# Two attentions: query tiles of stride four, four wide turning products, and value products moved ahead of a score

## The reference

```python
# L2: 8 heads of 16, softmax attention; the heads of a channel are added, then a raw reshape
p = softmax(einsum('bhsd,bhtd->bhst', q, k) / sqrt(dk))
att = einsum('bhst,bhtd->bhsd', p, v)
out = att.reshape(S, B, D, H).sum(axis=-1).reshape(B, S, D)
# L3: 16 heads of 8, scanned over blocks of 64 keys with a running maximum m;
#     l_new = chunk_sum * corr + chunk_sum, so the last block's correction enters the denominator
out = flash(Q, K, V).transpose(0, 2, 1, 3).reshape(B, S, E) @ out_w.T + out_b
```

## Time and profile before

| | us |
|---|---|
| median of 3 runs | 3012.55 (3006.28 to 3018.29) |
| profiled execution, its own time | 3009.39 |
| its span on the core | 3007.6 |
| `sa` head loop, about | 1266 to 1742 |
| `ba` head loop, about | 1934 to 2812 |

### The profile page before, as it was taken

One profiled execution on the slowest core, in us unless ns is written; L12 is line 12 of the kernel. 1 busy time (PEld: TensorE's weight loads), 2 busy tenths in 40 slices (PEclk: granted clock), 3 DMA queues, 4 the chain that ended last, 5 costly groups with the idle time before them and its releaser, 6 DMA issues.

```text
span 3007.6 us, 61281 instructions
## 1 busy us (share of the span) xinstructions
PE 2345.3 (78%) x19700; PEld 1301.3 (43%) x19752; DVE 1890.4 (63%) x3795; ACT 1308.9 (44%) x2628; POOL 507.1 (17%) x941
## 2 busy tenths in 40 slices
PE   4369958788887785499999955489999999999855
PEld 3246634666665432234444433133333333333434
DVE  5857565655554476376666645477777777777281
ACT  4211144333332202156666633166666666666322
POOL 4402320333332002011111101000000000000013
PEclk9655567889998697599999977599999999999676
DMA  2232200000000001411111001411111111111000
GB/s 64 75 100 64 66 22 0 7 0 0 0 0 1 7 0 45 143 31 28 27 27 27 22 3 49 137 28 32 28 30 32 27 32 32 27 32 27 2 16 28
DMA packets 146722, 98.97 MB, mean 33 GB/s; under 512 B 61150, under 2 KB 126055, under 8 KB 146602
## 3 DMA queue, kind: packets, MB, share of 16 engines
q1 hardware_dynamic: 146602, 97.35, 12.1%
HBM read 56.85 MB, written 39.85 MB: 32 GB/s over the span
## 4 chain that ended last, share of the span: by engine, by line
PE 57%; DVE 19%; issue 9%; ACT 6%; SPq 5%; POOL 2%; DMA 2%; DVEq 1%; ACTq 0%; POOLq 0%; PEldq 0%
PE psum L2056 10%; PE psum L2044 9%; PE psum L2033 9%; PE psum L2068 6%; SPq L1970 4%; DVE X L1281 2%; PE psum L645 1%; DVE tt_sp L1687 1%; PE psum L405 1%; DVE dn_arena L925 1%; ACT ba_pt L2132 1%; PE psum L634 1%; PE psum L668 1%; PE psum L1604 1%; DVE tt_tsp L1685 1%
## 5 line engine op out<-in xcount | busy, mean ns | idle before, releaser
L2262 DVE TENSOR_REDUCE ba_blockmax<-psum 128x16 f32<-128x1024 f32 x512 | 608.9, 1221 | 183.1 <-PE psum L2033 182.6
L2132 ACT ACTIVATE ba_pt<-psum 128x512 f32<-128x512 f32 x1024 | 541.5, 603 | 272.7 <-PE psum L2044 272.6
L2264 DVE TENSOR_REDUCE sa_negmax<-psum 128x1 f32<-128x1024 f32 x256 | 304.4, 1221 | 151.3 <-PE psum L2033 150.9
L2044 PE MATMUL psum<-ba_qs,ba_ks 64*128 64x512 bf16 x1024 | 339.5, 383 | 72.0 <-DVEq L59 50.9
L2033 PE MATMUL psum<-ba_ks,ba_qs 64*128 64x512 bf16 x1024 | 347.1, 423 | 38.4 <-DMA ba_ks<-ba_kstk 30.6
L2132 ACT ACTIVATE sa_pt<-psum 128x512 f32<-128x512 f32 x512 | 268.2, 602 | 194.1 <-PE psum L2044 120.4
L2056 PE MATMUL psum<-ba_pt,ba_vh 128*32 128x512 f32 x2048 | 278.4, 616 | 0.2 <-ACT ba_pt L2132 0.2
L2033 PEld LDWEIGHTS psum<-ba_ks,ba_qs 64*128 64x128 bf16 x1024 | 123.6, 146 | 306.5 <-issue 301.5
L2033 PE MATMUL psum<-sa_ks,sa_qs 96*128 96x512 bf16 x512 | 207.7, 411 | 41.1 <-DMA sa_ks<-sa_kstk 30.4
L2044 PE MATMUL psum<-sa_qs,sa_ks 128*128 128x512 bf16 x460 | 174.4, 383 | 10.2 <-DVEq L59 8.2
L2044 PEld LDWEIGHTS psum<-ba_qs,ba_ks 64*128 64x128 bf16 x1024 | 77.1, 93 | 174.4 <-issue 150.2
(11 more groups left out here) (477 smaller groups left out, 4165.3 us busy)
## 6 DMA issues: line engine op xcount, KB each, us to landing
ba_qs<-ba_qstk SPq DMA_DIRECT2D x128, 96.0 KB, 2.1
ba_ks<-ba_kstk SPq DMA_DIRECT2D x128, 96.0 KB, 2.2
sa_qstk<-sa_pq SPq DMA_DIRECT2D x48, 128.0 KB
sa_kstk<-sa_pk SPq DMA_DIRECT2D x48, 128.0 KB
sa_qs<-sa_qstk SPq DMA_DIRECT2D x32, 192.0 KB, 2.6
sa_ks<-sa_kstk SPq DMA_DIRECT2D x32, 192.0 KB, 2.7
ba_qstk<-ba_pq SPq DMA_DIRECT2D x48, 128.0 KB, 2.3
ba_kstk<-ba_pk SPq DMA_DIRECT2D x48, 128.0 KB, 2.3
```

The source lines that it names most:

```text
L2044: nc.tensor.matmul(bank(4 + slot), ks[b][K0:P, x_ * P:(x_ + 1) * P], qs[b][K0:P, h * HALF:(h + 1) * HALF], start=True, stop=True).then_inc ...
L2132: nc.scalar.activation(pt[2 * x_ + h][:, :], bank(4 + slot), ACT.Exp, scale=SCALE).then_inc(pt_in, 1)
L2262: ins = nc.vector.tensor_reduce(blockmax[g][:, r, :], src.rearrange("p (n s) -> p n s", s=BLOCK), AXX, ALU.max, negate=True)
L2264: ins = nc.vector.tensor_reduce(negmax[g][:, r:r + 1], src, AXX, ALU.max, negate=True)
```

## The change

Query tile r no longer holds the queries `a * 8 + r` but `(r // 4) * 512 + a * 4 + r % 4`. What follows from that: the row scores' weights have a column step of 4, the maxima go to `qs` by two DMAs of half a row for each part (four values, 8 bytes, from each partition), and four products with 128 weight columns (step 4) and both halves of `sel` as moving data take the place of the 16 of `turn_out`. In `sa` the result is no longer in the token order of `X`; SyncE moves it there by two DMAs into a new buffer `moved`, after the `maxima` of its body, and POOL's `add` waits for these. In `project_out` the copy's output order changes. Besides, in odd key tiles the value products are issued between the second row score and the second key-major score.

```diff
+    moved = [k.sb(f"{tag}_moved{g}", [P, D], ctx=ctx) for g in range(3)] if not blocked else None
...
             for z in range(3):
-                s.dma_start(qs[b][MR + z:MR + z + 1, :], mparts[b][:, z, :]).then_inc(m_in[b], 16)
+                for h in range(2):
+                    s.dma_start(qs[b][MR + z:MR + z + 1, h * HALF:(h + 1) * HALF],
+                                mparts[b][:, z, h * GROUP:(h + 1) * GROUP]).then_inc(m_in[b], 16)
...
                 maxima(n.at(1))
+            if not blocked and c != 0:
+                move(n.at(-1))
+
+        def move(n):
+            b = n.c % 3
+            s.wait_ge(normed, n.of(1, 1))
+            k.plain(s)
+            for h in range(2):
+                s.dma_start(moved[b][h * (P // 2):(h + 1) * (P // 2), :], onorm[b][:, h * GROUP:(h + 1) * GROUP, :]).then_inc(moved_in[b], 16)
...
         heads(s, body)
+        if not blocked:
+            move(Head(0, N - 1))
...
-            last = nc.tensor.matmul(bank(2 * slot + h), qs[b][0:KP, :].rearrange("p (a r) -> p r a", r=NTB)[:, r, :],
+            mine = qs[b][0:KP, r // GROUP * HALF:(r // GROUP + 1) * HALF].rearrange("p (a m) -> p m a", m=GROUP)[:, r % GROUP, :]
+            last = nc.tensor.matmul(bank(2 * slot + h), mine,
...
-            for r in range(NTB):
-                for h in range(2):
-                    lhsT = oT[n.c % 3][:, :].rearrange("p (a r) -> p r a", r=NTB)[:, r, :]
-                    last = nc.tensor.matmul(k.psum[h * 64:(h + 1) * 64, 4 + slot, r * V1:(r + 1) * V1], lhsT, sel[:, h, :],
-                                            start=True, stop=True, skip_group_check=True)
+            out = bank(4 + slot)[:, 0:NTB * V1].rearrange("p (h m e) -> p m h e", h=2, m=GROUP)
+            for m in range(GROUP):
+                last = nc.tensor.matmul(out[:, m, :, :], oT[n.c % 3][:, :].rearrange("p (a m) -> p m a", m=GROUP)[:, m, :], sel[:, :, :],
+                                        start=True, stop=True, skip_group_check=True)
...
-                    t.wait_ge(m_in[n.c % 3], n.third(48, 49))
+                    t.wait_ge(m_in[n.c % 3], n.third(96, 97))
...
                 for h in range(2):
                     if ahead:
                         rows_scores(lead, r, h)
+                    if h == 1 and x_ == 1 and c != 0:
+                        values(n.at(-1), 3)
+                    if h == 1 and x_ in (3, 5, 7):
+                        values(n, (x_ - 3) // 2)
                     key_scores(n, x_, h)
-                if x_ == 1 and c != 0:
-                    values(n.at(-1), 3)
-                if x_ in (3, 5, 7):
-                    values(n, (x_ - 3) // 2)
...
-            p.wait_ge(normed, n.of(1, 1))
+            p.wait_ge(moved_in[n.c % 3], n.third(32, 32))
...
-            nc.gpsimd.tensor_tensor(xs, xs, onorm[n.c % 3][:, :, :].rearrange("p r e -> p (r e)"), ALU.add).then_inc(added, 1)
+            nc.gpsimd.tensor_tensor(xs, xs, moved[n.c % 3][:, :], ALU.add).then_inc(added, 1)
...
-                dst = oT[b % 2][:, :].rearrange("d (p r) -> d r p", r=NTB)[:, g * GROUP:(g + 1) * GROUP, :]
+                dst = oT[b % 2][:, g * GT:(g + 1) * GT].rearrange("d (p m) -> d m p", m=GROUP)
```

More of the change, by code:

```diff
@@ L1912, in attention @@
     normed, all_done = mk("normed"), mk("all_done")
+    moved_in = many("moved_in", 3)
     layer = k.layers
@@ L2172, in split_max @@
             if n.c >= 3:
-                p.wait_ge(m_in[g], n.third(48, 1))
+                p.wait_ge(m_in[g], n.third(96, 1))
             k.plain(p)
```

## The result

The changed kernel takes **3076.2 us** (median of 4 runs, 3064.8 to 3081.3), against 3015.1 for the kernel before on the same chip: ratio **1.020** (95% interval 1.017 to 1.024). It is slower by 2%, some 61 us. The prediction was 3001, with a range of 2950 to 3032.

A forecast was written before the change was run, and what follows sets the result against it. `sa` was taken as bound by TensorE, `ba` by TensorE and its waits, with the maxima's chain becoming binding. The terms -34.2 + 2.7 + 3.6 + 18.6 - 2.0 = -11.3 took the median from 3012.5 to 3001 us, range 2980 to 3022 (outer 2950 to 3032).

The forecast's parts named there:

- I take T + 5.5: In `ba`, the row maximum of key tile 4 starts 5.5 us after T, the start of key tile 0.
- 0.1 to TensorE: In `ba`, TensorE starts 0.1 us after the last DMA of the maxima lands.
- 18.6: In `ba`, the longer maxima chain makes the period 13.7 against 13.39: +0.3 for each of 62 periods, +18.6 us.
- rival 2: In `ba`, dearer issues (0.7) or landings 0.5 later make the period 14.2, total 3033 us; chance 0.17.
- I take 0.97 ... 1.07 us saved a head: The turning products, 2.04 us before, take 0.97 us as 8 passes, saving 1.07 us a head.
- -34.2 us in `sa`: In `sa`, bound by TensorE, cheaper turning products save 1.07 us in each of 32 heads: -34.2 us.
- rival 3: The turning products do not get cheaper, `sa` stays at 14.36 a head, total 3037 us; chance 0.06.
- 0 (a column of step 4 costs what keeps the total): Lower bound on the turning products' saving a head: 0, if step-4 columns keep their total time unchanged.
- the order at 0: Issuing value products earlier in odd key tiles changes nothing: 0 in `sa`, hidden by the maxima wait in `ba`.
- The clock, named as a danger without a price: In `ba`, a granted clock under 1.00 because TensorE rests 2 us at a time would prove the forecast wrong.
- I take no change: Row scores' weight loads at step 4, bounded by 140 and 93 ns, were taken as unchanged.
- rival 4: Row weights at step 4 load in 93 ns, making `ba`'s period 13.5 and the total 2990 us; chance 0.12.

The follow-up runs named there:

- experiment 2: The changed kernel with the maxima written by three DMAs of a whole row, as before, instead of six: 3017.8 us, ratio 1.0036.
- experiment 4: The changed kernel with VectorE's `negative` issued after the row maximum of key tile 3 instead of key tile 4: 3021.7 us, ratio 1.0063.
- experiment 1: The changed kernel with each turning product reading 128 adjacent columns of `oT` as weights: 3070.4 us, ratio 1.021.
- experiment 9: The changed kernel with `negative` at key tile 3 and ScalarE's copy laying out adjacent columns for the turning products: 2948.2 us, ratio 0.978.
- experiment 3: The changed kernel with the value products put back behind the second key-major score: 3125.8 us, ratio 1.040.
- experiment 6: The kernel before with only the new order, value products of odd key tiles ahead of the second key-major score: 3022.6 us, ratio 1.0029.
- experiment 7: The kernel before with only the turning products in their new wide form, 128 queries each with stride four: 3014.7 us, ratio 1.0011.
- experiment 8: The kernel before with ScalarE's copy laying each query tile's 64 columns side by side, turning products still in halves: 2984.4 us, ratio 0.991.

## Why the prediction was wrong

**Right: the mechanism in `ba`.** The chain from row maximum through POOL and six DMAs binds, TensorE waits for it, and each DMA costs 0.60 whatever its bytes. 3.14 and the landing came out as written, five issues at 3.08 for 2.98. Taking the chain's length away, in two ways (experiments 2 and 4), takes most of the loss away. Here the rule cited from the Trainium skill (DMA: Bandwidth & Descriptors, Rules for kernel authors) held: splitting doubled SP's time for the issues of a head, 1.77 to 3.70 us, on the path.

**Wrong by its size: the chain.** "I take T + 5.5" measured 5.94; five issues took 0.10 more and "0.1 to TensorE" measured 0.26, so the period is 14.42 and not 13.72. The start's 0.44 is 27 us over 62 heads and the rest 16, and `ba`'s periods as a whole, 67 us against 18.6, are the largest part of the miss. The 0.1 was misread from its own row: 1280.09 + 2.0 against 1282.26 is 0.17. Of the 0.44, half shows in the timeline: I had added up TensorE's and VectorE's work without ScalarE, and the value products of key tile 3 (2536.80) stand behind the copy to `oT` (2535.88 to 2536.46), for which TensorE is idle 0.21. The rest is spread: the row score of key tile 3 starts at T + 3.19, not 3.05, and the last step to VectorE takes 0.63, not 0.5. The slope was known (the text put 62 us on each us of the period), and the forecast's own range allowed 0.2 for this term, while rival 2, which ends at 3033, put the excess on the DMAs and not here.

**Wrong: the turning products.** "I take 0.97 ... 1.07 us saved a head" took as nearest the row whose 128 weight columns are adjacent. They measured 1.86 (`sa`) and 1.94 (`ba`) from their start to the next product, and 0.88 to 0.97 with adjacent columns (experiments 1 and 9). A load of 128 fp32 columns takes 192 ns adjacent and 330 with a step; 64 take 138 and 217. The 64-column passes follow each other at 0.064 us, less than a third of one recorded load of 217, so their loads overlapped. An estimate that fits all four kernels: if the loads of the two halves run side by side, 16 pairs of 64 columns and 8 passes of 128 are the same 1024 columns in a row, 2.0 and 1.8 ns each with a step (2.04 and 1.86 us), 1.1 and 0.9 adjacent (1.1 and 0.88 to 0.97). No run takes the halves apart. -34.2 us in `sa` became -13, 21 us of the miss. This was rival 3's mechanism, at 0.06 far too low. My bound "0 (a column of step 4 costs what keeps the total)" was nearer to the value than what I took.

**Wrong: the order at 0.** It is worth 0.9 us a head beside six DMAs (experiment 3), and costs about 0.3 without them (experiment 6), part of it clock. The text had both halves of it (the wait for a bank, the delayed exponential) and called both hidden by the wait for the maxima. They were not: they lie between T and the row maximum of key tile 4, inside the chain that the wait belongs to. It is no term of the miss beside the others, as T + 5.5 was worked out for the new order. A wait hides only what is not upstream of it.

**The clock, named as a danger without a price.** In the changed kernel it goes to 0.88 or 0.77 in 30 of 58 heads and costs little, as the chain is the bound. But it caps the partial versions: experiments 1, 2, 4, 7 and 8 each lost 0.3 to 0.6 us a head of `ba` to it (their means against their heads at 1.00). The prediction looked for it after TensorE's wait for the DMA. In the changed kernel no fall comes there: all come as the turning products end.

**The rest.** First heads: forecast 3.6 in both attentions; the first turning products of `sa` start 7.4 us later than before (1308.9 against 1301.5), 4.2 of it the two waits above. `ba`'s last three periods: forecast -2, measured +6.3 (41.9 against 35.6). The last add: 2.7 forecast, 3.0. Row scores' weights: "I take no change" from a median of 140 (a mean of 146 in `ba`); in the changed kernel their mean is 112. By the Trainium skill (SBUF — State Buffer, Door 1) they should have shortened with two accesses to a 16-byte line; they did, but only part of the way to 93, and the 14.42 a head shows that this did not bring the period down to rival 4's 13.5. The span's +66.6 us, by the starts of turning products: +7.4 to `sa`'s first, -10 to its last (the second head's wait is in it), +7 to `ba`'s first, +71 to its last, -9 after it.

## What to carry to other kernels

- Before adding small DMAs to a chain, write that chain from its consumer back to its consumer one period earlier, with every engine in it, and price the terms from rows; work that lies ahead of its first link is part of it. Then look for a link it does not need: one `negative` behind a row maximum of another head was worth 1.4% here (1.020 to 1.006).
- Price a weight load by the layout of its columns, not by its count. ScalarE's copy, which has to write the tile anyway, laid the columns side by side at no cost and was worth 29 us alone. And let the cheaper operand take the step: moving columns in runs of four cost 7 to 15 ns a product, 0.1 to 0.2 us a head, while the same order by DMA took six instead of three and 0.5 us a head.
- When a stage on TensorE gets shorter but something else ends last, the rest grows and the clock may fall. Look at the granted clock head by head before counting the gain, and at what TensorE did just before it fell: here a wait (experiments 1 and 8) or the stepped turning products (experiment 2).
